# Adjacency counts of ten chunks gathered in one PSUM bank, chunk keys of 8 columns, sums of x on ScalarE

## What is computed

```
edge_index = jnp.stack([src, dst])            # 41250 edges, sorted by dst
x = x + _L0_gnn_ref(_layernorm(x, axis=-1), edge_index, W, b)
...
deg = jax.ops.segment_sum(jnp.ones_like(dst), dst, num_segments=n)    # after adding a loop per node
dis = jax.lax.rsqrt(jnp.maximum(deg, 1.0))
for l in range(W.shape[0]):
    h = x @ W[l]
    agg = jax.ops.segment_sum(h[src] * norm, dst, num_segments=n) + b[l]
    x = jax.nn.relu(agg)
```

## Time and profile before

| | |
|---|---|
| median of three runs | 893.17 us (892.9 to 894.33) |
| the profiled execution's own time | 891.18 us, its span 889.2 us |
| TensorE, matmul | 792.9 us busy (89% of the span) |
| TensorE, weight loads | 609.2 us (69%) |
| VectorE | 554.7 us (62%) |
| ScalarE | 332.1 us (37%) |
| GpSimd | 144.5 us (16%) |
| mean granted TensorE clock | 0.897 of 2.4 GHz |

### The profile page before, as it was taken

How to read it: one execution, slowest core, us unless ns; L and a number is a source line. 1 busy time by engine, 2 the same in 40 slices (tenths; PEclk the granted TensorE clock), 3 DMA queues, 4 the chain that set the end, 5 groups by cost and what they waited for, 6 DMA issues and landing times.

```text
span 889.2 us, 13389 instructions
## 1 busy us (share of the span) xinstructions
PE 792.9 (89%) x3864; PEld 609.2 (69%) x3865; DVE 554.7 (62%) x996; ACT 332.1 (37%) x624; POOL 144.5 (16%) x186
## 2 busy tenths in 40 slices
PE   4988799999999994986899976997989999999993
PEld 2444578888888872655788865787767777777761
DVE  7987491341242189799213478598567778877751
ACT  2567251341251112435221222333245555655541
POOL 2000000000000030000000420111314453555421
PEclk9555689999999997897999985997999999999997
DMA  7400000000000001000010302100989869865532
GB/s 178 146 1 1 2 1 0 1 1 1 1 1 0 5 26 50 1 1 1 0 48 1 113 1 91 25 1 1 341 292 346 227 163 306 310 192 88 144 69 35
DMA packets 32292, 71.37 MB, mean 80 GB/s; under 512 B 4387, under 2 KB 4637, under 8 KB 32243
## 3 DMA queue, kind: packets, MB, share of 16 engines
q1 hardware_dynamic: 24480, 53.31, 17.4%
q0 software_dynamic: 6272, 14.68, 8.3%
q10 hardware_dynamic: 1491, 2.73, 0.9%
HBM read 96.53 MB, written 12.72 MB: 123 GB/s over the span
## 4 chain that ended last, share of the span: by engine, by line
PE 76%; DVE 14%; issue 4%; ACT 3%; ACTq 1%; DMA 1%; DVEq 0%; POOL 0%; POOLq 0%
PE PS L1069 21%; PE PS L1099 9%; PE PS L1308 9%; PE PS L1355 8%; PE PS L1000 6%; PE PS L1192 5%; PE PS L1302 4%; PE PS L1138 3%; PE PS L1340 3%; ACT CTR L717 2%; PE PS L1286 1%; DVE XN L1425 1%; PE PS L1317 1%; PE PS L1043 1%; PE PS L1245 1%
## 5 line engine op out<-in xcount | busy, mean ns | idle before, releaser
L1069 PE MATMUL PS<-CTR,YH 125*128 125x500 f32 (+1 forms) x480 | 164.3, 357 | 2.3 <-DVE YL L1606 2.3
L1069 PE MATMUL PS<-CTR,YL 125*128 125x500 f32 (+1 forms) x480 | 163.8, 356 | 0.0
L1069 PEld LDWEIGHTS PS<-CTR,YH 125*128 125x128 f32 x480 | 91.7, 191 | 15.6 <-DVE YL L1606 2.6
L1069 PEld LDWEIGHTS PS<-CTR,YL 125*128 125x128 f32 x480 | 91.7, 191 | 13.0
L1000 PE MATMUL PS<-ET 125*128 125x130 f16 x494 | 71.7, 300 | 17.0 <-ACT CTR L717 9.5
L1926 DVE TENSOR_TENSOR W1L<-WB,W1H 128x1152 fp32r<-128x1152 f32 x56 | 74.0, 1356 | 14.0 <-issue 7.2
L1355 PE MATMUL PS<-WB,YF 128*128 x168 | 80.1, 615 | 2.6 <-issue 1.9
L1633 DVE TENSOR_TENSOR ZL<-PS,ZH 128x500 fp32r<-128x500 f32 (+1 forms) x36 | 21.1, 591 | 90.4 <-ACT ZH L775 90.4
L1000 PEld LDWEIGHTS PS<-ET 125*128 125x128 f16 x494 | 39.4, 121 | 50.0 <-ACT CTR L717 29.3
L1308 PE MATMUL PS<-W1H,XGH 128*128 128x384 f32 x168 | 73.4, 437 | 0.0
L948 ACT CAST W1H<-WB 128x1152 fp32r x56 | 64.2, 1151 | 16.1 <-issue 10.6
(11 more groups left out here) (374 smaller groups left out, 1596.9 us busy)
## 6 DMA issues: line engine op xcount, KB each, us to landing
WB<-in_w SPq DMA_DIRECT2D x28, 1536.0 KB
WB<-in_w SPq DMA_DIRECT2D x28, 768.0 KB
WB<-in_b SPq DMA_DIRECT2D x28, 384.0 KB
X<-in_x SPq DMA_DIRECT2D x1, 2240.0 KB
xn_dram<-XN SPq DMA_DIRECT2D x1, 2240.0 KB
WNEXT<-in_W SPq DMA_DIRECT2D x2, 1024.0 KB, 9.5
SR<-in_sw SPq DMA_DIRECT2D x1, 1536.0 KB, 7.6
out<-X ACTq DMA_DIRECT2D x1, 1120.0 KB
```

The source lines that it names most:

```text
L1069: mm = nc.tensor.matmul(dest, lhs, rhs, start=(t == 0 and h == 0), stop=(t == NT - 1 and h == 1))
```

## The change

Ten chunks of a batch now share one PSUM bank of 10 x 51 columns. A matmul of one row of zeros clears it (510 columns); each chunk then adds its 8 key columns per tile (80 columns, keys relative to its own first target) at its offset in the window, which TensorE reads from a register; chunk 0 is at offset 0. The first chunk of the next batch adds one more column (10 columns) once its one-hots are there. Two register loads per batch, one of nine values and one of one, are issued in the middle of the batch before. ScalarE copies 10 x 50 columns once per batch. The third one-hot, `bn_stats` and `bn_aggr` go; ScalarE forms sums of x in batches 2 to 11 and of squared deviations in batches 14 to 23; VectorE forms XHAT, after the last batch. The checks follow batch 2's one-hots, the flag batch 5's. The wait of the degree matmuls for `counts_ready` is left to the slow path. A semaphore of a later stage (`minus_ready`) is replaced by a second count on `loops_ready`. The diff, cut to its core:

```diff
@@ -36,14 +36,19 @@
 NG = NCH // OWN
 BATCH = 5
 LOADS = 8
-STATS_AT = 4
-DEV_AT = STATS_AT + 10
-XHAT_AT = DEV_AT + 4
 NBAT = NG // BATCH
+PER = OWN * BATCH
+CHECK_AT = 2
+FLAG_AT = 5
+SUMS_AT = 2
+SQUARES_AT = 14
+DEV_AT = 26
 RING = 3
-WIN = 12
-SLOTS = WIN + 1
+SLOTS = 8
 KEYS = NT * SLOTS
+BWIN = 50
+BKEYS = NT * (BWIN + 1)
+LAST_OFF = BWIN + 1 - SLOTS
 CPG = 5
 NSG = NCH // CPG
...
@@ ScalarE @@
+            def window_places(b):
+                row = place_i[0:1, b:b + LOADS]
                 return nc.values_load_multi_w_load_instructions(
+                    row, engines=(mybir.EngineType.Activation,), min_val=0, max_val=CW - BWIN,
+                    skip_runtime_bounds_check_because="DVE clamps the table to 0..CW - BWIN")[1]
 
             following = window_places(0)
+            for b in range(NBAT):
+                if b % LOADS == 0:
                     places = following
+                if b % LOADS == LOADS // 2 and b + LOADS // 2 < NBAT:
+                    following = window_places(b + LOADS // 2)
+                act.wait_ge(group_done, b + 1)
+                if b:
+                    act.wait_ge(placed, b)
+                nc.scalar.copy(CTR[0:NP, :, bass.ds(places[b % LOADS], BWIN)],
+                               PS[0:NP, b % 6, 0:BKEYS].rearrange("p (t w) -> p t w", t=NT)[:, :, 1:BWIN + 1]
                                ).then_inc(placed, 1)
+                t = b - SUMS_AT
+                if 0 <= t < NT:
+                    if t == 0:
+                        act.wait_ge(load["x"], 32)
+                    if t >= 2:
+                        act.wait_ge(sums_ready, t - 1)
+                    nc.scalar.activation(val[0:NP, t % 2, :], X[0:NP, t, :], ACT.Identity,
+                                         accum_out=sums[0:NP, 0, t:t + 1]).then_inc(sums_ready, 1)
+                t = b - SQUARES_AT
+                if 0 <= t < NT:
+                    act.wait_ge(mean_neg, 1)
+                    act.wait_ge(sums_ready, NT + max(t - 1, 0))
+                    nc.scalar.activation(val[0:NP, t % 2, :], X[0:NP, t, :], ACT.Square, bias=minus[0:NP, t:t + 1],
+                                         accum_out=sums[0:NP, 1, t:t + 1]).then_inc(sums_ready, 1)
+                if b == DEV_AT:
                     sqrt_of_var(0)
...
@@ TensorE @@
+            pe.wait_ge(const_done, 6)
+            pe.wait_ge(windows_ready, 1)
+            windows = lambda b: PS[0:128, b % 6, 0:BKEYS].rearrange("p (t w) -> p t w", t=NT)
+
+            def offsets(b):
+                late = "DVE clamps both tables to the window"
+                within = nc.values_load_multi_w_load_instructions(
+                    off_i[0:1, b * (PER - 1):(b + 1) * (PER - 1)], engines=(mybir.EngineType.PE,), min_val=0,
+                    max_val=LAST_OFF, skip_runtime_bounds_check_because=late)[1]
+                past = nc.values_load_multi_w_load_instructions(
+                    next_i[0:1, b:b + 1], engines=(mybir.EngineType.PE,), min_val=0, max_val=BWIN,
+                    skip_runtime_bounds_check_because=late)[1]
+                return within, past[0]
+
+            def first_column(b, past):
+                k = (b + 1) % RING
+                return nc.tensor.matmul(windows(b)[:, :, bass.ds(past, 1)], oh_lo[k][0:CHUNK, 0, :, 0],
+                                        oh_key[k][0:CHUNK, 0, :, 0].rearrange("p (t w) -> p t w", t=NT)[:, :, 0:1],
+                                        start=False, stop=True)
+
+            following = offsets(0)
+            for b in range(NBAT):
+                pe.wait_ge(onehot_ready, b + 1)
+                if b:
+                    first_column(b - 1, past).then_inc(group_done, 1)
+                within, past = following
+                if b >= 6:
+                    pe.wait_ge(placed, b - 5)
+                nc.tensor.matmul(PS[0:128, b % 6, 0:BKEYS], iota_lo[0:1, :, 0], blank[0:1, :], start=True, stop=False)
+                for j in range(PER):
+                    if j == PER // 2 and b + 1 < NBAT:
+                        following = offsets(b + 1)
+                    at_col = windows(b)[:, :, bass.ds(within[j - 1], SLOTS)] if j else windows(b)[:, :, 0:SLOTS]
+                    mm = nc.tensor.matmul(at_col, oh_lo[b % RING][0:CHUNK, j // OWN, :, j % OWN],
+                                          oh_key[b % RING][0:CHUNK, j // OWN, :, j % OWN].rearrange("p (t w) -> p t w", t=NT),
+                                          start=False, stop=(j == PER - 1 and b == NBAT - 1))
+                if b == FLAG_AT - 1:
+                    pe.wait_ge(bad_ready, 1)
+                    nc.tensor.matmul(PS[:, 6, 0:1], ones[0:NP, :], bad[0:NP, 0:1], start=True, stop=True
+                                     ).then_inc(bad_sum, 1)
+            mm.then_inc(group_done, 1)
...
-            pe.wait_ge(placed, NG)
-            pe.wait_ge(counts_ready, 1)
+            pe.wait_ge(placed, NBAT)
...
@@ VectorE: tables and keys @@
+            link(v.tensor_copy(wbase[:, 0:NCH], PS[:, 7, 0:NCH]))
...
+            link(v.tensor_scalar(edge[0:1, :], wbase[0:1, 0:NCH:PER], 1.0, 0.0, ALU.add, ALU.max))
+            v.tensor_scalar(place_i[0:1, 0:NBAT], edge[0:1, :], float(CW - BWIN), None, ALU.min)
+            offs_of = offs[0:1, :].rearrange("p (b j) -> p b j", j=PER)
+            link(v.tensor_tensor(offs_of, wbase[0:1, 1:NCH + 1].rearrange("p (b j) -> p b j", j=PER),
+                                 wbase[0:1, 0:NCH:PER].rearrange("p (b o) -> p b o", o=1).to_broadcast([1, NBAT, PER]),
+                                 ALU.subtract))
+            v.tensor_scalar(off_i[0:1, :].rearrange("p (b j) -> p b j", j=PER - 1), offs_of[:, :, 0:PER - 1], 0.0,
+                            float(LAST_OFF), ALU.max, ALU.min)
+            v.tensor_scalar(next_i[0:1, :], offs_of[:, :, PER - 1], 0.0, float(BWIN), ALU.max, ALU.min
+                            ).then_inc(windows_ready, 1)
+
+            link(v.tensor_tensor(key16[0:CHUNK, :, :].rearrange("p g x -> p (g x)"), where[0:CHUNK, :],
+                                 wbase[0:CHUNK, 0:NCH], ALU.subtract))
...
@@ VectorE: one-hots, checks, loop @@
-                return v.tensor_tensor(oh_next[b % RING][0:CHUNK].rearrange("p g (n x) -> p g n x", x=2),
...
+                return v.tensor_tensor(oh_key[b % RING][0:CHUNK],
...
+            def check_order():
+                v.tensor_tensor(where[0:CHUNK, :], dstf[0:CHUNK, :], wbase[0:CHUNK, 0:NCH], ALU.is_ge)
...
+            def check_windows():
+                link(v.tensor_tensor(holds[0:1, 0:NCH], wbase[0:1, 1:NCH + 1], wbase[0:1, 0:NCH], ALU.subtract))
...
+            def set_flag():
+                dve.wait_ge(bad_sum, 1)
+                link(v.tensor_scalar(bad[:, 2:3], PS[:, 6, 0:1], 0.5, None, ALU.is_ge))
+                link(v.scalar_tensor_tensor(out=bad[0:1, 2:3], in0=bad[0:1, 3:4], scalar=0.5, in1=bad[0:1, 2:3],
+                                            op0=ALU.is_lt, op1=ALU.max))
+                link(v.tensor_copy(flag_i[0:1, 0:1], bad[0:1, 2:3]))
+                v.tensor_copy(WH[:, 0, 0:128], ones[:, :]).then_inc(flag_ready, 1)
             for b in range(NBAT):
                 if b >= RING:
+                    dve.wait_ge(group_done, b - RING + 1)
                 onehots(b).then_inc(onehot_ready, 1)
+                if b == CHECK_AT:
+                    check_order()
+                    check_windows()
+                if b == FLAG_AT:
+                    set_flag()
+                if b == SQUARES_AT - 1:
+                    dve.wait_ge(sums_ready, NT)
+                    v.tensor_scalar(minus[0:NP, :], sums[0:NP, 0, :], -1.0 / D, None, ALU.mult).then_inc(mean_neg, 1)
+                if b == DEV_AT - 1:
+                    dve.wait_ge(sums_ready, 2 * NT)
+                    v.tensor_scalar(mv[0:NP, :, 1], sums[0:NP, 1, :], 1.0 / D, EPS, ALU.mult, ALU.add).then_inc(var_ready, 1)
+
+            dve.wait_ge(sd_ready, 1)
+            link(v.reciprocal(rstd[0:NP, :], sd[0:NP, :]))
+            for t in range(NT):
+                v.tensor_scalar(XHAT[0:NP, t, :], X[0:NP, t, :], minus[0:NP, t:t + 1], rstd[0:NP, t:t + 1],
+                                ALU.add, ALU.mult).then_inc(val_ready, 1)
```

More of the change, by code:

```diff
@@ L229, in build @@
         rstd = sb("rstd", [128, NT])
-        shift = sb("shift", [128, NT])
+        sums, minus = sb("sums", [128, 2, NT]), sb("minus", [128, NT])
         dis = sb("dis", [128, NT])
@@ L995, in _ @@
             nc.tensor.matmul(PS[:, 7, 0:NCH], ones[0:1, :], dstf[0:1, 0:NCH], start=True, stop=True).then_inc(base_read, 1)
[L997 to L1015, removed]
@@ L1017, in _ @@
-            pe.wait_ge(bad_ready, 1)
-            nc.tensor.matmul(PS[:, 6, 0:1], ones[0:NP, :], bad[0:NP, 0:1], start=True, stop=True).then_inc(bad_sum, 1)
+            pe.wait_ge(const_done, 6)
[10 more added lines that the diff above has]
+                return within, past[0]
@@ L1049, in _ @@
             with pe.If(slow > 0):
+                pe.wait_ge(counts_ready, 1)
```

(38 more changed lines are left out.)

78 lines of the change are left out of this document (19 added, 59 removed).

## The result

The changed kernel takes **921.26 us** (median of four runs, 918.85 to 923.78) against 893.75 for the kernel before beside it (892.9 to 896.3): ratio 1.030, 95% interval 1.027 to 1.034. It is slower by 27.5 us; forecast was 883.6, faster, with a range to 898. The profiled execution took 918.85 us, its span 916.9.

What follows compares the result with a forecast made beforehand. TensorE's queue was to bind at 2.30 us a batch; 11.7 + 73.6 + 1.3 + 0.9 + 0.5 + 1.4 put the degrees at 89.4, 9.6 us earlier, so 883.6 us from 893.17; range 870 to 898.

Steps and rivals of the forecast that it cites:

- VectorE per batch: One-hots in the adjacency count stage: 1.23 us a batch instead of 1.90, so VectorE is no longer the bound.
- Register instructions: Offset arithmetic on TensorE's queue: ten a batch at 0.125 us each, 1.25 us (1.0 to 1.5).
- One-value load: Second register load of each batch on TensorE's queue: 0.36 us including the step to the next instruction.
- Static pairs: Two weight-load and matmul pairs without register offset on TensorE's queue: hardly any cost, 0.02 us a batch.
- The array's share: TensorE's twelve matmuls and their weight loads per batch: up to 1.8 us at 1.2 GHz, partly under the loads.
- The nine-value load: First register load of each batch on TensorE's queue: 0.61 us plus 0.06 to the next instruction, 0.67.
- The sum: All terms up to the degree matmuls: they start at 89.4 us against 98.96, 9.6 us earlier.
- The stall behind the checks: TensorE waits for VectorE's batch 3 one-hots, as the checks follow batch 2's: 0.9 us.
- Register loads dearer: Rival, chance 0.12: both loads on TensorE's queue cost 0.49 us, not 0.30; 2.68 a batch, 895.8 us, slower.
- Loads that don't block: Rival, chance 0.08: TensorE's queue goes on during a load; about 1.6 us a batch, 22 us more off, 861.
- Matmuls cost the queue time too: Rival, chance 0.06: each of twelve matmuls holds TensorE's queue 0.046 us; 2.85 us a batch, 901 us, slower.
- The clock and later waits: Rival, chance 0.06: the gain is eaten by the clock or a later wait, 889 us.

Runs made afterwards that it cites:

- e8: e1 with the sums of x back on VectorE as ten bn_stats and the twenty ScalarE activations left out: 889.12 us (0.996).
- e1: Changed kernel with offset-table rows of 12 words instead of 9, so every nine-value load begins on a multiple of 16 bytes: 888.61 us (0.994).
- e4: Changed kernel without both register loads and all register offsets, chunks at fixed columns, counts not the graph's: 857.82 us (0.960).
- e6: Changed kernel with two chunks sharing one register offset, 10 columns per pair, one aligned load of five words and five register instructions a batch: 860.82 us (0.966).
- e7: e1 with one aligned load of twelve words in place of the loads of nine and one: 878.07 us (0.986).

## Why the prediction was wrong, point by point

**What bounds.** Right: TensorE's queue binds after the change, VectorE and ScalarE wait for it.

**VectorE per batch**, 1.23 forecast: 1.22 (one-hots of batches 1 and 2 start at 11.41 and 12.63 us). **ScalarE:** the copy has the 0.58 that was read from a copy of that shape, and the sum, for which I took 0.1 between nothing and 0.26, is 0.19. The activation itself takes 0.63 (sum of x) and 0.72 (squares) in place of 0.82, so that the 0.92 for both together came out at 0.82 and 0.91:

```profile
L718 ACT CAST CTR<-PS 125x500 f32 x33 | 19.2, 583 | 76.7 <-PE PS L1022 75.8 <-PE PS L1039 0.8
...
L733 ACT ACTIVATE val<-X,minus 125x512 f32<-125x512 f32 x10 | 7.2, 722 | 0.0
...
L1552 DVE TENSOR_SCALAR XHAT<-X,minus,rstd 125x512 f32<-125x512 f32 x10 | 4.7, 540 | 0.0
...
L727 ACT ACTIVATION_READ_ACCUMULATOR val<-X 125x1 f32 x10 | 1.9, 192 | 0.0
```

XHAT, ten of 0.54, was hidden as forecast, and so were the sums (e8).

**Register instructions**, ten of 0.125: 0.124 apart in the trace, one or two in a batch 0.155. **One-value load**, 0.36: 0.306 and 0.06 behind it. **Static pairs**, 0.02: nothing that shows. From the register instruction of the first column (L1022) to the next one it is 0.124 as well, with three pairs of weight load and matmul in that step in place of one; and e1's batch of 2.55 to 2.57 leaves at most 0.05 beside 1.24 + 0.91 + 0.37. The array's share, put at up to 1.8, is 1.42 (e4).

**The nine-value load is the step that failed.** "Eight values there 0.55: 0.038 per further value. Nine values: 0.30 + 8 x 0.038 = 0.61, plus 0.06 = 0.67." It was 2.23 in 24 of 32 batches and 0.91 in eight. The slope was drawn through two rows, a load of one and ScalarE's load of eight, and both are on the cheap side of a rule that I didn't know: ScalarE's table starts at word 0 and is read in steps of eight words, so that each of its loads is on a multiple of 16 bytes and ends with a full group. Two accesses were read as eight values. Nine values lie just past the last full group and, in three batches of four, off the boundary. For the upper bound I added 0.19 to it, from a load of one value behind a wait, which makes 0.86; nothing in the rows bounded what a value more can cost from above, and the bound should have been one that did: nine times the 0.30 of a load of one, 2.7 us. With it the upper end would have been 2.30 + 2.1 = 4.4 us a batch, 883.6 + 32 x 2.1 = 951 us.

The Trainium skill ("Runtime: NRT & Kernel Launch", "Instruction fetch mechanics") gives TENSOR_LOAD about 200 ns per register, also in bulk; it tells this of loads from HBM, and the table here lies in SBUF. Carried over, it gives nine values an estimated 1.8 us and the batch 3.5 us; I did not weigh it, and it would have spoken against this change. The runs come near it for words off the boundary (0.23 us for each word more) and not for aligned groups (twelve words in 0.85 us, 0.07 each).

**The sum.** In the order of the forecast: first matmul 11.7, was 11.55; 32 batches 73.6, were 113.8 with the flag in them; the last batch and the tail 2.7, were 2.4 (125.31 to 127.69). The stall behind the checks (0.9) did not come, as TensorE took 1.58 us a batch more than forecast; in e6, whose queue is fast, it came with 2.8 us. The flag was 0.35 for 0.5. In all 127.7 for 89.4, 38.3 us later: the load of nine alone makes 24 x 1.56 + 8 x 0.24 = 39.4, and the stall that did not come takes 0.9 off. In e1, with an aligned table, the remaining error is in the main that of 0.24 us a batch: degrees at 95.7 and 888.6 us for the forecast 883.6, and 4.7 us below the kernel before beside it where 9.6 were forecast.

**The rivals.** "Register loads dearer" had the right place and sign, for a reason that is not so: it added 0.19 to each load for cold code, and the load of one stayed at 0.306. The first load of nine in the kernel is dearer by about as much (1.045 against 0.844 in e1), the later ones are not. "Loads that don't block" is out: the next instruction of the queue comes 2.23 us after a load of 2.17 has begun, 0.36 after one of 0.30. "Matmuls cost the queue time too" is out with the 0.124 that a step takes, whether one pair lies in it or three. The clock and later waits took nothing: from the degrees to the end 788 to 792 us in the kernel before, the changed one and every experiment but e4 (794.6, on counts that are not the graph's; its profiled execution was also the slowest of its four, 860.8 against 856.6 to 858.8), which was not followed up.

**Not settled:** why three accesses take 0.85 and not 0.77 as two steps of 0.23 would make them, and whether a load that begins off the boundary could ever use groups behind it (nine words from byte 8 of a group don't: 2.17).

## What to carry to other kernels

A table that is read into registers wants each load to begin on a multiple of 16 bytes and to end with a full group of four words: pad the rows, and read the padding too. Price a register load by its accesses (0.31 us and about 0.25 for each further one here; other counts than one, five, eight, nine, ten and twelve were not tried), not by its values, and when a slope goes through two rows, look where those rows lie in memory before it is used for a third. Where one queue binds, the next step is to ask it for less: sharing an offset between two chunks cost 20 more columns for each chunk on the array and gave, with the second load gone too, 28 us over the aligned table and 17 over the single load of twelve words. The faster the queue, the more the position of other work (the checks) matters: batch 3 comes late by 0.1 us in e1, by 1.2 in e7 and by 2.8 in e6.

## What the runs showed of the hardware

- TENSOR_LOAD of 4-byte words from SBUF, TensorE's queue: one 0.306 us, five aligned 0.58, nine aligned 0.845, ten aligned 1.08, twelve aligned 0.848, nine not aligned 2.17. ScalarE's queue, eight aligned: 0.55.
- Register instructions (FUSED_REGOPS, 46 ns each) follow each other every 124 ns in TensorE's queue, with one pair of weight load and matmul between them or with three.
- The sum of an activation is an instruction of its own, ACTIVATION_READ_ACCUMULATOR, 192 ns.
- The profile's column for the granted clock reads 1.00 through the stage of the changed kernels, and 0.50 in the kernel before, but the array's pace there is that of the 1.2 GHz level: 20 columns more for each of ten chunks take 0.17 us a batch (1.42, 1.59, 1.75), 0.83 ns a column. The first sixteen degree matmuls, 500 columns each in 6.61 us at 127.69, give the same 0.83 ns under a column that reads 1.00.
